# The order of columns in which the expanded down weight is written to HBM

## What is computed

```python
def spline_reconstruct(control_points, out_size, in_size):
    n = out_size * in_size
    idx, f = _catmull_rom_grid(control_points.shape[0], n)
    p0, p1, p2, p3 = (control_points[idx[k]] for k in range(4))
    w = 0.5 * (2.0 * p1 + (p2 - p0) * f + ... * f2 + ... * f3)
    return w.reshape(out_size, in_size)
gate_w = spline_reconstruct(gate_cp, 8192, 2048)
up_w   = spline_reconstruct(up_cp,   8192, 2048)
down_w = spline_reconstruct(down_cp, 2048, 8192)
x = x + layernorm(attention(layernorm(x)))
inter = silu(h @ gate_w.T) * (h @ up_w.T)      # h = layernorm(x)
x = x + layernorm(inter @ down_w.T)
```

## Time and profile before

| what | us |
|---|---|
| median of 2 runs | 4550.2 |
| the two runs | 4482.84, 4617.57 |
| the profiled execution | 4492.96 |
| its span on core 4, the slowest | 4491.3 |
| gu stage | about 15 to 697 |
| stage B | 697 to 1375 |
| attention | 1375 to 2039 |
| stage D | 2039 to 2256 |
| down stage | 2256 to 2897 |
| stage E | 2897 to 4491 |

### The profile page before, as it was taken

One profiled execution on the slowest core, in us unless ns is written; L12 is line 12 of the kernel. 1 busy time (PEld: TensorE's weight loads), 2 busy tenths in 40 slices (PEclk: granted clock), 3 DMA queues, 4 the chain that ended last, 5 costly groups with the idle time before them and its releaser, 6 DMA issues.

```text
span 4491.3 us, 41712 instructions; the slowest of 8 cores (4470.9 to 4491.3 us)
## 1 busy us (share of the span) xinstructions
PE 2953.6 (66%) x12832; PEld 1170.9 (26%) x12832; DVE 1439.9 (32%) x1876; ACT 926.0 (21%) x1519; POOL 531.5 (12%) x968
## 2 busy tenths in 40 slices
PE   3444442799996676768312222189998947999895
PEld 0111111344442111113200000044443323444332
DVE  5666667322222434340644444311000022000002
ACT  3444443000002333431212222200000021000001
POOL 5555550000000000000021111000000000000000
PEclk9999999999997778779655555589999978999997
DMA  7888884544441000005479999944433444444344
GB/s 160 194 202 192 193 192 149 81 75 76 77 75 58 29 28 20 29 19 75 142 117 121 129 130 126 119 150 154 155 141 113 136 145 154 155 150 150 108 136 141
DMA packets 604456, 538.51 MB, mean 120 GB/s; under 512 B 306352, under 2 KB 521392, under 8 KB 593712
## 3 DMA queue, kind: packets, MB, share of 16 engines
q1 hardware_dynamic: 484816, 397.55, 30.8%
q0 software_dynamic: 119424, 138.29, 21.4%
HBM read 405.40 MB, written 134.22 MB: 120 GB/s over the span
## 4 chain that ended last, share of the span: by engine, by line
PE 50%; DMA 17%; DVE 15%; SPq 11%; issue 4%; ACT 2%; POOL 1%; DVEq 0%; ACTq 0%; POOLq 0%
PE pq L689 12%; SPq L160 11%; PE pgE L1081 10%; PE puE L1087 10%; PE pdE L1130 6%; DMA wdsb<-wbuf_d 5%; DMA gi<-gct 4%; DVE gwo L443 4%; PE pav L226 3%; PE prow L222 3%; PE psc L824 3%; PE po L903 2%; DVE rs L859 2%; DMA wbuf_d<-dwo 2%; DVE colsb L236 2%
## 5 line engine op out<-in xcount | busy, mean ns | idle before, releaser
L1081 PE MATMUL pgE<-x2f,wgsb 128*128 128x512 bf16 x2048 | 779.1, 380 | 13.9 <-DMA wusb<-wbuf_u 13.9
L1087 PE MATMUL puE<-x2f,wusb 128*128 128x512 bf16 x2048 | 779.0, 380 | 0.0
L689 PE MATMUL pq<-x2T,wq 128*128 128x512 bf16 x2560 | 554.1, 380 | 11.3 <-DMA wq<-wqkvT 11.3
L422 PE MATMUL pguA<-Ug,atsb 16*128 16x512 bf16 x512 | 267.6, 598 | 405.7 <-DVE Ug L387 333.7
L1130 PE MATMUL pdE<-actsb,wdsb 128*128 128x512 bf16 x2048 | 460.4, 381 | 56.6 <-DMA wdsb<-wbuf_d 55.9
L551 PE MATMUL pdnA<-Ud,atsb 16*128 16x512 bf16 x256 | 133.8, 598 | 489.5 <-DVE dwo L569 263.9
L443 DVE CAST_PREDICATED gwo<-gm,pguA 128x512 bf16<-128x512 uint8 x512 | 353.6, 691 | 166.4 <-ACT gwo L438 120.4
L438 ACT CAST gwo<-pguB 128x512 bf16<-128x512 f32 x512 | 300.4, 587 | 354.0 <-PE pguB L422 300.6
L1102 DVE TENSOR_TENSOR actsb<-silsb,puE 128x512 bf16<-128x512 bf16 x128 | 88.0, 687 | 816.7 <-ACT silsb L1097 816.7
L689 PEld LDWEIGHTS pq<-x2T,wq 128*128 128x128 bf16 x2560 | 250.8, 98 | 314.4 <-issue 13.4
L835 ACT ACTIVATE pT<-psc 128x512 bf16<-128x512 f32 x384 | 229.3, 597 | 328.1 <-PE psc L824 324.5
(11 more groups left out here) (82 smaller groups left out, 2218.0 us busy)
## 6 DMA issues: line engine op xcount, KB each, us to landing
wgsb<-wbuf_g SPq DMA_DIRECT2D x128, 512.0 KB, 3.7
wusb<-wbuf_u SPq DMA_DIRECT2D x128, 512.0 KB, 4.6
wdsb<-wbuf_d SPq DMA_DIRECT2D x128, 512.0 KB, 3.7
gi<-gct POOLq DMA_DIRECT2D x512, 64.0 KB, 6.0
wbuf_g<-gwo SPq DMA_DIRECT2D x64, 512.0 KB, 11.3
wbuf_u<-gwo SPq DMA_DIRECT2D x64, 512.0 KB, 13.0
wbuf_d<-dwo SPq DMA_DIRECT2D x32, 1024.0 KB, 40.4
wq<-wqkvT POOLq DMA_DIRECT2D x24, 1024.0 KB, 10.1
```

What stands on the lines that cost most here:

```text
L422: t.matmul(pp[:, :], at_sb[u_:u_ + 16, :], U[b][u_:u_ + 16, cc:cc + 512], start=True, stop=True, tile_position=(u_, 0)))
L689: t.matmul(pq[bi][:, :], wq[(o // 2) % 2][:, h * 256 + (o % 2) * 128: h * 256 + (o % 2) * 128 + 128], x2T[:, h * S + g * 512:h * S + g * 5 ...
L1081: t.matmul(pg[bi][:, :], wg[o % 4][:, h * 128:h * 128 + 128], x2f[:, h * 512:h * 512 + 512], start=(h == 0), stop=(h == 15)))
L1087: t.matmul(pu[bi][:, :], wu[o % 4][:, h * 128:h * 128 + 128], x2f[:, h * 512:h * 512 + 512], start=(h == 0), stop=(h == 15)))
```

## The change

The store of a chunk of the down weight is written as one run of 4,096 columns for each partition, and the host orders the columns of taps, offsets and mask so that these are the right ones: the whole array is ordered with ic outermost and o innermost, and chunk c holds ic = 2c and 2c+1 for all 2,048 output rows. The contents of `wbuf_d` after the stage, its layout, the shapes of all loads, the number of instructions on every engine and all waits are the same.

```diff
-                    od = DCH // 64
                     sch.wait("Y", evmark[c * NCG + NCG - 1])
                     stok[c] = sch.dma(
                         "Y",
-                        AP(wbuf_d, c * od,
-                           [[64 * D, 128], [D, 64], [1, od]]),
-                        AP(WO[c % 4], 0, [[DCH, 128], [od, 64], [1, od]]),
+                        AP(wbuf_d, c * DCH, [[64 * D, 128], [1, DCH]]),
+                        WO[c % 4][:, :],
                         f"dws{c % 4}")
@@
 def _perm_dn():
     if "dn" not in _TPR:
-        p = np.arange(DCH).reshape(DCH // 64, 64).T.ravel()
-        _TPR["dn"] = (np.arange(NBLK).reshape(-1, DCH)[:, p]).ravel()
+        _TPR["dn"] = (np.arange(D)[None, :] * 64
+                      + np.arange(64)[:, None]).ravel()
     return _TPR["dn"]
```

## The result

The changed kernel runs in 4337.6 us (median of 11 runs), the kernel before in 4499.8 (median of 10). The ratio is 0.9653, 95% interval 0.9628 to 0.9678: faster by 3.5%. Both medians count some slower executions, in which cores ran at a lower granted clock; the ratio is that of the others alone. The profiled execution took 4334.8 us against 4492.96, 158.2 us less; forecast were 197.7.

The account below looks back on a forecast made before the run. DMA engines bind the down stage, half their time on stores in 8,192 pieces. From 2340.3, 24 intervals at 13.0 and three at 10.3, plus the final store, end at 2699.1, saving 197.7 off 4492.96: 4295 us, range 4225 to 4385.

Parts of the forecast that it names:

- The store's DMA time: Down stage: 128 rows of 8,192 bytes take 2.9 us a chunk in place of 9.8, gaining 220 us of DMA time.
- SP's issue: Down stage: a store of 128 rows no longer holds SP, whose median issue was 16.2 us; issues under 4 us.
- Rival D: Down stage: SP stays held at 16.2 us a store despite fewer pieces; 77 us more, 4372; chance 0.06.
- Stage E at nothing: Stage E's reads of wbuf_d keep the same addresses, so its cost was put at nothing.
- The software queue: Down stage: taps, offsets, mask and copies keep the stage average of 9.6 us a chunk, 307 us in all.
- the early stretch: Down stage, 2300 to 2340 us: the software queue took 8.5 us a chunk, giving a sum of 11.4.
- rival B: Down stage: the chain of load and copy landings becomes the bound, 15.1 us an interval; 50 us more, 4345; chance 0.12.
- The engines' share: Down stage: 12.5 us of DMA time a chunk divided by the 97% reached before, 12.9, rounded to 13.0 us an interval.
- The last three intervals: End of the down stage: no loads left to share with, so 10.3 us each, 30.9 us together.
- Rival A: Down stage: software packets shrink without tiny store packets, VectorE's loop binds at 10.3 us; 65 us less, 4230; chance 0.15.
- Rival C: Down stage: long store packets starve the copies, kernel slower; break-even at landings of 53.5 us, 4583 at 65; chance 0.01.
- Landings of the store: Down stage: the store of a chunk lands in 6 to 15 us after issue.

Follow-up runs that it names:

- tapports: Changed kernel with the five down-stage tap rows at partitions 0, 4, 8, 12, 16 of dct instead of 0 to 4, offsets at 20 to 51: 4243.0 us.

## Why the prediction was right, and where it was off

The forecast was faster, 4295 us in a range of 4225 to 4385; measured were 4337.6 and, in the profiled execution, 4334.8. Direction and place held, and the store's part of the mechanism; the saving was 158 us and not 198. The step that failed is the software queue's term and the share it was divided by.

- *The store's DMA time.* Forecast 2.9 us a chunk and 94 us in all; measured 2.8 and 88.9. Right.
- *SP's issue.* "Should no longer hold SP": median 0.32 us, the longest 5.6, and gone from the chain. Right. Rival D is out, and pieces of 512 bytes show the issue falling with their number. The number isn't all: the same 8,192 pieces held SP 16.2 us in the kernel before and 9.6 with taps read from HBM.
- *Stage E at nothing.* 2.3 us shorter. Right.
- *The software queue, the term that failed.* I took the average of the stage before, 9.6 us a chunk, over the early stretch's 8.5. It came out at 330.4 / 32 = 10.3. I held the queue's busy time to be work that stays the same, gave the sum a lower value (8.5) and no higher one, and named a rise only as a sign of rival B. It moves with the place of the rows of `dct` alone: 330.4 us against 273.9 in tapports. That faster chunks made the crowd denser is argued and not shown, but the kernels with crowded taps fit it: 7.1, 7.4, 7.6, 7.7 and 7.9 us per MB at intervals of 17.9, 14.3, 13.8, 13.7 and 11.7. The copies were known to be slow for their size, 141 against 357 GB/s; the prediction said so, and then kept the sum as it was.
- *The engines' share.* I divided by the 97% of the stage before as if it were what the engines can reach. It is no ceiling: the queues' shares add up to 116% in the old store with taps from HBM, and the share is 1.01 in the middle of tapports (the row is below). In the middle of the changed stage it is 0.93. The other kernels with crowded taps and a new store have 0.89 to 0.91 between 2400 and 2600 us, those without the crowd 1.01 to 1.05. With 10.3 + 2.8 = 13.1 over 0.93 the interval is 14.1, and 14.1 is what the 24 middle intervals had: (2682.9 - 2344.3) / 24. Against 13.0 that is 27 us.
- *The last three intervals*, put at 10.3 each since no loads are left: they took 2725.9 - 2682.9 = 43.0 us, 12 more, for `Ud` waited for its copies twice more. Together with 1 us in the first four intervals this accounts for the 40 us between forecast and result.
- *Luck.* Adding the queues' busy times came within 1.1 us of the middle interval. With the old store and taps from HBM the same sum gives (296.9 + 366.1) / 32 = 20.7 us where the interval was 16.1. That the method served here is in part luck.
- *Rival A*, short packets slow the copies and the interval falls to 10.3 without them: out, the copies got slower. But short packets do slow them where the taps are out of the way: the same 13,312 packets took 296.9 us beside the old store and 274.2 beside the new one.
- *Rival B*: its number, 4345, is nearest to the result, but for the wrong reason. With the landings measured, 17.2 and 15.3 us, its own formula gives (17.2 + 15.3 + 3.2) / 3 = 11.9 us and not 13.8, and the deeper pipeline, which would have broken a chain of landings, changed next to nothing. The argument against it failed too: the landings got longer.
- *Rival C*: landings of copy and load summed to 32.5 us, not 53.5.
- *Landings of the store*: forecast 6 to 15 us, measured 22.2. Wrong, and harmless, with four buffers and 13.8 us an interval. With rows spread they are 13.3.

The window 2400:2700 of the changed kernel, then 2400:2600 of tapports (PE, PEld, DVE, ACT, POOL busy, PEclk, DMA share, GB/s):

```profile
2400.00:2700.00 300.00, 90.76 (x336) 23.84 (x336) 165.03 (x191) 98.58 (x168) 78.47 (x148) 0.50 0.93 168
2400.00:2600.00 200.00, 75.08 (x280) 19.80 (x280) 135.76 (x155) 80.47 (x138) 64.43 (x121) 0.50 1.01 208
```

## What to carry to other kernels

When an engine that only issues transfers stands in the chain, count the pieces of its transfers; if the order of the data on the host is free, give it the order in which the device writes long rows. Before putting a queue's busy time into a sum, hold its GB/s against another stage's: where it is far lower for rows of the same size, some of the time may be waiting, and will not stay the same when the pace or the place changes. Where a small tile is read many times by copies, try its rows on partitions further apart; it costs an offset in an access pattern, and here it gave 78 us of the stage.

## What the runs showed of the hardware

- Where in SBUF a handful of rows lies changes the DMA time of a stage by 56 us of 330, at equal packets and bytes: rows read four-fold at partitions 0 to 4 against 0, 4, 8, 12, 16 (with the offsets at 5 to 36 against 20 to 51).
- The packets' times of two queues overlap: their shares of the 16 engines' time add up to 97% in the kernel before and to 116% with the old store and taps from HBM. The same 262,656 store packets took 312.8 and 366.1 us.
- SP is held longer by a store in more pieces: medians of 0.32, 6.0 and 16.2 us for 128, 2,048 and 8,192 pieces of the same megabyte, beside the same traffic on the software queue. With other traffic there (taps from HBM) 8,192 pieces held it 9.6 us.
- A transfer to HBM of 8 KB rows that landed in 5.4 us where the engines were busy for half of the time took 22.2 us beside the crowded copies and 13.3 beside the spread ones.
- A wait of the queue of GpSimd is put down to VectorE in the changed kernel (`POOL di <- DVE dwo`), although the count it needed from VectorE was reached long before; at 2340.2 us the load of `dct` was 23 us old, within the 26.7 that the longest took to land, and is the likelier cause. This was read from the order of the issues and not tested.
